# Second pass of a four-layer kernel: its first sequence written out ahead of the loop, weight pieces split inside that sequence's steps, twelve pieces staged ahead

## The chip, the core and the metric

The kernel runs on one core of one Trainium2 chip. The metric is the device time of one execution in microseconds (us), the median of several runs.

## What is computed

Eight sequences of 512 rows and 512 features pass through four layers one after the other: an adapter (layer 0), an attention block with a feed-forward part (layer 1), a feed-forward expert (layer 2) and a finite-difference step on the 512x512 grid that each sequence then is (layer 3). Cut to what matters here:

```python
# layer 1, behind the attention: x is (8, 512, 512)
h = _ln(x) * g2 + beta2
x = x + _gelu2(h @ W1 + b1) @ W2 + b2            # W1 512x2048, W2 2048x512, the same for all sequences
# layer 2: one of 8 experts for each sequence
h = gelu(x @ Wi[expert_idx] + bi)
r = h @ Wo[expert_idx] + bo + x
y = layer_norm(r) * gamma + beta
# layer 3: f = y as a grid
Af, Bf = A_grid * f, B_grid * f
df = -(grad(Af[0], 1) + grad(Af[1], 2)) + 0.5 * (grad2(Bf[0], 1) + grad2(Bf[1], 2) + ...)
out = maximum(f + df * dt, 0)
```

Matmuls of layers 1 and 2 are made with 16-bit operands: each float32 operand is split into a high and a low half (`_hi`, `_lo`), and each product is three matmuls (hi by hi, lo by hi, hi by lo; L1371 to L1373, 128x512 each).

## The kernel before, in words

**Two passes.** `attention_pass` runs layer 0 and the attention over all eight sequences (a hardware loop, L413 on SyncE) and stores its result `x2` to memory (`x_rows`). `ffn_pass` then runs the rest of layer 1, layer 2 and layer 3. Each pass is a block: all engines meet at its end. ScalarE, which issues the stores of `x2`, waits until all have landed (the last line of its part of the first pass) before it ends its block. Order of work on each engine is the order in which the code is written; engines wait for each other by semaphores.

**A sequence of the second pass** is 32 steps (`STEPS`, L1037), 16 of layer 1 (`n` below 16) and 16 of layer 2. In step `n` TensorE makes `up(n)` (12 matmuls into one of four banks), and then `down(n - 2)` (12 matmuls into the four accumulators; L1406 to L1444). ScalarE makes the gelu (L1512), VectorE splits its result into halves (L1686, L1687), which `down(n)` needs. Layer 2's weights come in 16 chunks of 512 KB: SyncE loads each into one of two buffers (L1257), ScalarE and VectorE split it (L1519, L1692) in steps 4, 6, 8 to 14 and later ones (`CHUNK`, L1044). In the middle of a sequence and at its end TensorE transposes the next activations (L1437, L1378).

**Layer 3 runs one sequence behind.** In the loop's body for sequence `it` the engines also normalise and difference the sequence before: `norm3`, `alpha` and `beta` on VectorE, grid products on GpSimd (L1298, L1305 to L1308), four times five matmuls on TensorE (`run_stencil`, L1423, L1357) and a store. So that the body is the same for every `it`, the first one does all of this on a tile `f` of zeros (memsets L1321, L1322), and its output rows are overwritten later. The last sequence's layer 3 stands behind the loop.

**Start of the second pass.** W1 and W2 are loaded in 16 pieces of 512 KB (`weight_pieces`). Four are loaded while the first pass ends, into slots 0 to 3 of a buffer `stage` of six slots (L442), and sequence 0's `x2` into slots 4 and 5 (L444). The second pass loads the vectors (L1241, L1243), normalises `x2` (L1554 to L1647), transposes it, and splits the 16 pieces ahead of the loop: high half on ScalarE (L1496), low half on VectorE (L1656). A slot is reloaded when its piece has been split (L1246). `up(0)` waits for four pieces and the split activations (L1394, L1402), `down(0)` for all sixteen (L1411):

```python
def down(n):
    k = n % NF
    if n == 0:
        pe.wait_ge(w_split, len(PIECES))
    pe.wait_ge(g_split, 1 + it * STEPS + n + 1)
```

GpSimd adds a bias to `x2` in four instructions (`move_x2`, L1312) as soon as the normalised rows are there. 24 matmuls on the identity (L1388) follow the first transposes on TensorE.

## Time and profile before

| | |
|---|---|
| median of 3 runs | 2598.64 us (2595.83 to 2599.11) |
| the profiled execution: time of the run | 2600.86 us |
| its span, first to last instruction | 2598.7 us |
| mean granted TensorE clock | 0.988 of full speed |
| busy: TensorE / VectorE / ScalarE / GpSimd | 2502.8 / 2011.6 / 1149.0 / 1050.5 us |
| first pass, second pass (by the block's end) | 0 to 1106 us, 1106 to 2598.7 us |

Times below are microseconds from the start of the span. A row of the timeline is: start, duration, engine, line, operation, output<-inputs with their shapes, count, and in brackets how long the engine had been idle before it and who released it. Matmuls are pipelined, so a row shows 0.38 us for one while they follow each other at some 0.216 us.

### The profile page before, as it was taken

The page shows a single profiled execution, that of the slowest core. Times are in us where ns is not written, and L with a number is a line of the kernel's source. Part 1 is how long each engine was busy: PE and PEld are TensorE (multiplying, and loading weights), DVE is VectorE, ACT ScalarE, POOL GpSimd, SP SyncE. Part 2 cuts the span into 40 slices and gives each one's busy share as a digit, 9 for nine tenths or more (in the row PEclk, how much of TensorE's full clock was granted, in tenths as well). Part 3 has the DMA queues.
Part 4 walks back from the last instruction along what each step waited for, and adds up shares of the span by engine and source line. Part 5 has one row for each costly group of instructions (what it writes and reads, how often), then busy time and mean ns, then how long its engine had stood idle before and what let it go on. Part 6 is the DMA issues. An engine that isn't in the chain of part 4 may idle for free.

```text
span 2598.7 us, 47184 instructions
## 1 busy us (share of the span) xinstructions
PE 2502.8 (96%) x14583; PEld 1240.8 (48%) x14583; DVE 2011.6 (77%) x3863; ACT 1149.0 (44%) x2189; POOL 1050.5 (40%) x887
## 2 busy tenths in 40 slices
PE   7999999999999999959999999999999999999997
PEld 5455555555555555534444444444444444444443
DVE  7777777777777777788868788688677886986787
ACT  3676767676767676733323222223232232232331
POOL 1464646464646464524324144143242350431330
PEclk8999999999999999979999999999999999999998
DMA  6444444445444444443222222242133222321440
GB/s 209 136 153 156 154 154 156 151 155 153 156 154 154 155 153 153 155 159 126 90 98 87 102 99 89 70 138 90 63 113 110 98 78 82 122 90 58 131 155 27
DMA packets 155507, 320.56 MB, mean 123 GB/s; under 512 B 17474, under 2 KB 23234, under 8 KB 155218
## 3 DMA queue, kind: packets, MB, share of 16 engines
q1 hardware_dynamic: 145426, 299.13, 35.1%
q10 hardware_dynamic: 9792, 17.83, 1.9%
q8 instruction: 151, 2.47, 0.4%
q14 instruction: 138, 1.13, 0.1%
HBM read 298.85 MB, written 17.86 MB: 122 GB/s over the span
## 4 chain that ended last, share of the span: by engine, by line
PE 51%; DVE 4%; issue 1%; ACT 1%; DMA 0%; DVEq 0%; ACTq 0%
PE ffn_bank L1371 16%; PE ffn_bank L1372 16%; PE ffn_bank L1373 16%; PE ffn_bank L1357 2%; DVE g2T_hi L1686 1%; PE ffn_bank L1437 1%; DVE g2T_lo L1687 1%; PE ffn_bank L1378 1%; DVE w_lo L1656 1%; DMA stage<-in_W 0%; PE ffn_bank L1466 0%; ACT g L1512 0%; DVE stage L1631 0%; DVE stage L1613 0%; DVE w_hi L1734 0%
## 5 line engine op out<-in xcount | busy, mean ns | idle before, releaser
L1000 DVE CUSTOM_DVE_ANT_0 tiles<-bank,stage 128x512 f32<-128x512 f32 x512 | 324.0, 687 | 81.1 <-PE bank L628 76.4
L792 ACT ACTIVATE tiles<-tiles,nmax 128x512 f32<-128x512 f32 x512 | 363.3, 713 | 47.1 <-DVE nmax L1000 47.0
L508 POOL TENSOR_TENSOR stage<-stage,mask_add 128x1024 f32<-128x1024 f32 x128 | 272.2, 2137 | 211.2 <-DMA stage<-in_bias 189.3
L651 PE MATMUL bank<-ident,tiles 128*128 128x128 f32 x2048 | 300.4, 280 | 18.9 <-ACT v L758 5.9
L1686 DVE CAST g2T_hi<-g 128x512 f16<-128x512 f32 x256 | 180.0, 703 | 176.7 <-ACT g L1512 169.3
L651 PEld LDWEIGHTS bank<-ident,tiles 128*128 128x128 f32 x2048 | 222.7, 140 | 179.5 <-issue 84.0
L1687 DVE TENSOR_TENSOR g2T_lo<-g,g2T_hi 128x512 f16<-128x512 f32 x256 | 259.6, 1014 | 8.8
L1298 POOL TENSOR_TENSOR stage<-grid,f 128x512 f32<-128x512 f32 x96 | 158.8, 1680 | 254.0 <-DVE f L1572 109.6
L1512 ACT ACTIVATE g<-ffn_bank,bi 128x512 f32<-128x512 f32 x128 | 87.9, 687 | 333.5 <-PE ffn_bank L1373 308.9
L778 ACT ACTIVATE pT<-bank 128x512 f32<-128x512 f32 x256 | 150.9, 589 | 152.1 <-PE bank L651 152.1
L1312 POOL TENSOR_TENSOR x<-x2n,b 128x512 f32<-128x512 f32 x32 | 39.5, 1269 | 439.3 <-DVE f L1714 439.3
L1371 PE MATMUL ffn_bank<-w_hi,g2T_hi 128*128 128x512 f16 x512 | 194.9, 381 | 14.6 <-DVE g2T_lo L1687 14.4
L1305 POOL TENSOR_TENSOR stage<-grid,f 128x512 f32<-128x512 f32 x64 | 96.1, 1521 | 268.1 <-DVE stage L1623 151.0
L1692 DVE SCALAR_TENSOR_TENSOR wl_lo<-stage,wl_hi 128x1024 f16<-128x1024 f32 x128 | 199.8, 1561 | 0.1
L1371 PE MATMUL ffn_bank<-x3T_hi,w_hi 128*128 128x512 f16 x512 | 194.0, 379 | 4.5 <-DVE x3T_lo L1653 3.4
L1371 PE MATMUL ffn_bank<-wl_hi,g2T_hi 128*128 128x512 f16 x512 | 194.1, 379 | 3.1 <-DVE g2T_lo L1687 3.1
L1372 PE MATMUL ffn_bank<-w_lo,g2T_hi 128*128 128x512 f16 x512 | 194.7, 380 | 0.0
L1373 PE MATMUL ffn_bank<-w_hi,g2T_lo 128*128 128x512 f16 x512 | 194.6, 380 | 0.0
L1371 PE MATMUL ffn_bank<-x3T_hi,wl_hi 128*128 128x512 f16 x512 | 194.2, 379 | 0.0
L1372 PE MATMUL ffn_bank<-wl_lo,g2T_hi 128*128 128x512 f16 x512 | 194.0, 379 | 0.0
L1373 PE MATMUL ffn_bank<-wl_hi,g2T_lo 128*128 128x512 f16 x512 | 194.0, 379 | 0.0
L1373 PE MATMUL ffn_bank<-x3T_hi,w_lo 128*128 128x512 f16 x512 | 194.0, 379 | 0.0
(289 smaller groups left out, 5230.5 us busy)
## 6 DMA issues: line engine op xcount, KB each, us to landing
stage<-in_bias SPq DMA_DIRECT2D x256, 512.0 KB, 4.3
stage<-in_W_l SPq DMA_DIRECT2D x128, 512.0 KB, 3.3
grid<-in_grids SPq DMA_DIRECT2D x160, 256.0 KB, 3.4
xin<-in_x SPq DMA_DIRECT2D x36, 256.0 KB, 4.0
out<-stage ACTq DMA_DIRECT2D x36, 256.0 KB, 2.0
x_rows<-tiles ACTq DMA_DIRECT2D x32, 256.0 KB, 3.0
stage<-in_W SPq DMA_DIRECT2D x16, 512.0 KB, 4.8
x2n<-x_rows SPq DMA_DIRECT2D x8, 1024.0 KB, 9.0
```

The lines of the kernel that those rows point to most:

```text
L508: pool.tensor_tensor(bias[:, n % NB, :, :], bias[:, n % NB, :, :], mask_add[:, u % T, :].unsqueeze(1).to_broadcast([P, 2, S]), ALU.add).th ...
L651: mm = pe.transpose(bank[:, t * P:(t + 1) * P], tiles[:, 4 * (u % NR) + i, t * P:(t + 1) * P], ident[:, :])
L778: act.activation(pT[:, (u // 2) % 2, i, :, (u % 2) * P:(u % 2 + 1) * P], bank[:, :].rearrange("p (t q) -> p t q", t=T), ACT.Copy).then_inc ...
L792: act.activation(tile, tile, ACT.Exp, scale=-1.0, bias=nmax[:, u % 2, i:i + 1], accum_out=rsum[:, j, h:h + 1]).then_inc(prob_ready, 1)
L1000: dve.tensor_tensor_reduce(tiles[:, 4 * (u % NR) + i, :], bank[:, :], bias[:, half % NB, i % 2, :], -1.0, 3.0e38, ALU.add, ALU.min, nmax[: ...
L1298: pool.tensor_tensor(prod[:, i, :], grid[:, i, :], f[:, t, :], ALU.mult).then_inc(alpha_prod, 1)
L1371: pe.matmul(out, w[0], x[0], start=first, stop=False)
L1372: pe.matmul(out, w[0], x[1], start=False, stop=False)
L1373: return pe.matmul(out, w[1], x[0], start=False, stop=last)
L1686: link(dve.tensor_copy(gT[0][:, n % 4, :], g32[:, n % 2, :]))
L1687: dve.tensor_tensor(gT[1][:, n % 4, :], g32[:, n % 2, :], gT[0][:, n % 4, :], ALU.subtract)\
L1692: dve.scalar_tensor_tensor(out=wl[1][:, k % NW, :], in0=raw[:, k % 2, :], scalar=WS, in1=wl[0][:, k % NW, :], op0=ALU.mult, op1=ALU.subtract)\
```

## The change

- The first sequence of the second pass is written out ahead of the loop, without layer 3 (there is no sequence before it); the loop runs over the other seven, with layer 3 of the sequence before. In place of each of the four `run_stencil` of the first sequence TensorE only signals the bank. The memsets of `f` and `l2_rows` go.
- Twelve pieces are staged ahead instead of four: 4 to 11 go into a buffer `late` of eight slots, the memory of the first pass's transposed probabilities `pT`, when the last product that reads those is done (`pv_done`). In the second pass the same memory holds `x2n`, `x2` and the halves `vsp`, `msp`.
- Before `up(0)` only pieces 0 to 3 are split. Pieces 4 and 5 are split in step 0, 6 to 15 in steps 1 to 10 (`PIECE_AT`), and `down(n)` waits only for the piece that it reads, `up(8)` for the first eleven. Pieces 12 and 13 are loaded into slots 2 and 3 of `stage`, pieces 14 and 15 into slots 4 and 5 when `move_x2` has read `x2` there.
- `move_x2` on GpSimd now waits until eight pieces are split, since its output lies in the slots of pieces 6 and 7.
- The vectors `g2`, `beta2`, `b1`, `dt`, `b2` and `idx` are loaded in the first pass, behind the first load of `ada` and ahead of its loop.

```diff
-NS = 4
+NS = 12
+PIECE_AT = {0: (4, 5), **{n: (n + 5,) for n in range(1, 11)}}
...
-    return w1[:C] + w2[:2] + w1[C:] + w2[2:]
-
-
-def staged(stage, i):
-
-    v = stage[:, i % NS, :]
-    return v.rearrange("p (k n) -> p k n", k=2) if C <= i < C + 2 or i >= 2 * C + 2 else v
-
-
-def attention_pass(nc, a, ada_rows, x2_dram, stage, stage_in):
+    return w1[:C] + w2[:2] + w1[C:C + 2] + w2[2:3] + w1[C + 2:] + w2[3:]
+
+
+def staged(stage, late, i, at):
+
+    v = stage[:, i, :] if i < C else late[:, i - C, :] if i < NS else stage[:, i - NS + 2, :]
+    return v if isinstance(at, tuple) else v.rearrange("p (k n) -> p k n", k=2)
+
+
+def staged_in(stage_in, i):
+
+    if i < NS:
+        return stage_in[i], 16
+    return stage_in[(2, 3, NS, 0)[i - NS]], 32
...
-        pT = sb("pT", [P, 2, 4, T, 2 * P], F32)
+        pT = late[:, :, :].rearrange("p (v i) (t q) -> p v i t q", v=2, t=T)
...
+            for dst, src in vectors(a, cols):
+                sp.dma_start(dst, src).then_inc(cols_in, 16)
...
-            for i, (src, _) in enumerate(weight_pieces(a)[:NS]):
-                sp.dma_start(staged(stage, i), src).then_inc(stage_in[i], 16)
+            pieces = weight_pieces(a)
+            for i in range(C):
+                sp.dma_start(staged(stage, late, i, pieces[i][1]), pieces[i][0]).then_inc(stage_in[i], 16)
             sp.wait_ge(x2_out, 1 + 64)
-            sp.dma_start(stage[:, NS:NS + 2, :].rearrange("p n (h s) -> p (n h) s", h=2),
+            sp.dma_start(stage[:, C:C + 2, :].rearrange("p n (h s) -> p (n h) s", h=2),
                          x2_dram[0].rearrange("(t p) d -> p t d", p=P)).then_inc(stage_in[NS], 16)
+            sp.wait_ge(pv_done, 1 + B * (NQ // 2))
+            for i in range(C, NS):
+                sp.dma_start(staged(stage, late, i, pieces[i][1]), pieces[i][0]).then_inc(stage_in[i], 16)
...
+        x2n, x2 = (late[:, i:i + 2, :].rearrange("p n (h d) -> p (n h) d", h=2) for i in (0, 2))
...
+        vsp, msp = ([late[:, i + j, :].bitcast(F16).rearrange("p (t d) -> p t d", t=T) for j in range(2)] for i in (4, 6))
...
-            for i, (src, _, _) in enumerate(PIECES):
-                if i >= NS:
-                    sp.wait_ge(w_split, i - NS + 1)
-                    sp.dma_start(staged(stage, i), src).then_inc(stage_in[i % NS], 16)
+            for i in range(NS, len(PIECES)):
+                if i < NS + 2:
+                    sp.wait_ge(w_split, i - NS + 3)
+                else:
+                    sp.wait_ge(x2b_ready, T)
+                signal, _ = staged_in(stage_in, i)
+                sp.dma_start(PIECES[i][1], PIECES[i][0]).then_inc(signal, 16)
             sp.dma_start(dmat[:, :, :], a["dmat"]).then_inc(dmat_in, 16)
             sp.dma_start(halo_w[:, :], a["halo"]).then_inc(dmat_in, 16)
-            sp.wait_ge(w_split, len(PIECES))
             sp.wait_ge(idx_clipped, 1)
-            with sp.Fori(0, B) as it:
-                e = sp.value_load(idx[0:1, bass.ds(it, 1)], min_val=0, max_val=NE2 - 1)
+
+            def sequence(it):
...
                 def load_rows():
-                    sp.wait_ge(f_ready, it * T + T)
+                    if not is_first(it):
+                        sp.wait_ge(f_ready, it * T)
                     sp.dma_start(bi[:, :], a["bi"][e]).then_inc(rows_in, 16)
                     sp.dma_start(l2_rows[:, :, :], a["rows2"][e].partition_broadcast(P)).then_inc(rows_in, 16)

                 def load_next_x2():
                     sp.wait_ge(x2b_ready, it * T + T)
+                    if is_first(it):
+                        sp.wait_ge(w_split, C + 2)
                     nxt = (it + 1) % B
...
+                loads += [(ALPHA[1], 2, load_rows, ()), (ALPHA[1], 3, load_next_x2, ())]
+                if not is_first(it):
+                    loads += [(ALPHA[t - 1] if t else -1, 1, stencil_load, (sp, it - 1, "alpha", t)) for t in range(T)]
+                    loads += [(BETA[t - 1] if t else ALPHA[-1], 1, stencil_load, (sp, it - 1, "beta", t)) for t in range(T)]
+                    loads += [(ALPHA[-1], 2, load_halo, ())]
...
+            sequence(0)
+            with sp.Fori(1, B) as it:
+                sequence(it)
...
-            pool.memset(f[:, :, :], 0.0).then_inc(zeroed, 1)
-            pool.memset(l2_rows[:, :, :], 0.0).then_inc(zeroed, 1)
             pool.memset(halo[:, :, :].rearrange("p t d -> p (t d)").bitcast(F32), 0.0).then_inc(zeroed, 1)
-            pool.wait_ge(vec_in, 16 * len(COLS))
+            pool.wait_ge(cols_in, 16 * len(cols))
             pool.wait_ge(h2_ready, T)
+            pool.wait_ge(w_split, 2 * C)
             for t in range(T):
                 move_x2(pool, x2_first, t)
...
-                    if n in (0, NF // 2):
-                        pe.wait_ge(w_split, C if n == 0 else 2 * C + 2)
+                    if is_first(it) and n in (0, NF // 2):
+                        pe.wait_ge(w_split, C if n == 0 else HALF_OF_W1)
...
-                    if n == 0:
-                        pe.wait_ge(w_split, len(PIECES))
+                    if is_first(it) and n in PIECE_OF_ROW:
+                        pe.wait_ge(w_split, PIECE_OF_ROW[n] + 1)
                     pe.wait_ge(g_split, 1 + it * STEPS + n + 1)
...
                     bank = claim(pe, it, ("L3", t))
-                    pe.wait_ge(alpha_done, it * T + T)
-                    pe.wait_ge(halo_in, it * 128 + 128)
+                    if is_first(it):
+                        pe.sem_inc(full_of(("L3", t)), 1)
+                        return
+                    pe.wait_ge(alpha_done, it * T)
+                    pe.wait_ge(halo_in, it * 128)
...
+            def piece_hi(i):
+                _, src, hi, _ = PIECES[i]
+                act.wait_ge(*staged_in(stage_in, i))
+                act.activation(hi, src, ACT.Copy, scale=WS).then_inc(w_hi, 1)
+
+            for i in range(C):
+                piece_hi(i)
+            act.wait_ge(cols_in, 16 * len(cols))
+            for c in range(C):
+                act.wait_ge(first_full, c + 1)
+                act.activation(xT[0][:, c, :], psum[c][:, :], ACT.Copy).then_inc(hi_done, 1)
+
...
+                    if is_first(it):
+                        for i in PIECE_AT.get(n, ()):
+                            piece_hi(i)
...
-            dve.wait_ge(idx_in, 16)
+            dve.wait_ge(cols_in, 16 * len(cols))
...
+            def piece_lo(i):
+                _, src, hi, lo = PIECES[i]
                 dve.wait_ge(w_hi, i + 1)
-                dve.scalar_tensor_tensor(out=lo, in0=staged(stage, i), scalar=WS, in1=hi,
-                                         op0=ALU.mult, op1=ALU.subtract).then_inc(w_split, 1)
-            dve.wait_ge(zeroed, 2)
-            before = links[0]
-
-            with dve.Fori(0, B) as it:
-                links[0] = 0
-                link = chained(it * LINKS_B + before)
-                prev = (it + (B - 1)) % B
+                dve.scalar_tensor_tensor(out=lo, in0=src, scalar=WS, in1=hi, op0=ALU.mult, op1=ALU.subtract).then_inc(w_split, 1)
+
+            piece_lo(0)
+            for c in range(C):
+                dve.wait_ge(hi_done, c + 1)
+                dve.tensor_tensor(xT[1][:, c, :], psum[c][:, :], xT[0][:, c, :], ALU.subtract).then_inc(h2T_split, 1)
+            for i in range(1, C):
+                piece_lo(i)
+
...
+                    if is_first(it):
+                        for i in PIECE_AT.get(n, ()):
+                            piece_lo(i)
...
+                    if not is_first(it):
+                        if n < 3:
+                            norm3(link, prev, n)
+                        if n in ALPHA:
+                            alpha(link, prev, ALPHA.index(n))
+                        if n in BETA:
+                            beta(link, prev, BETA.index(n))
...
+            sequence(0, link)
+            before = links[0]
+            with dve.Fori(1, B) as it:
+                links[0] = 0
+                sequence(it, chained((it - 1) * LINKS_B + before))
...
+        late = ctx.enter_context(nc.sbuf_tensor("late", [P, 8, 2 * D], F32))
```

**SyncE, from the last loads of the first pass over the block's end.** Before:

```order
L442 DMA stage<-in_W 128x1024 x4
L444 DMA stage<-x_rows 128x4x512
L153 UNCONDITIONAL_BRANCH
L1239 UNCONDITIONAL_BRANCH
L1241 DMA idx<-in_idx 1x8
L1243 DMA g<-in_g 128x512
L1243 DMA beta<-in_beta 128x512
L1243 DMA b<-in_b 128x16
L1243 DMA dt<-in_dt 128x8
L1243 DMA b<-in_b 128x512
L1247 DMA stage<-in_W 128x2x512 x2
L1247 DMA stage<-in_W 128x1024 x4
```

Now:

```order
L460 DMA stage<-in_W 128x1024 x4
L462 DMA stage<-x_rows 128x4x512
L466 DMA late<-in_W 128x2x512 x2
L466 DMA late<-in_W 128x1024 x2
L466 DMA late<-in_W 128x2x512
L466 DMA late<-in_W 128x1024 x2
L466 DMA late<-in_W 128x2x512
L168 UNCONDITIONAL_BRANCH
L1261 UNCONDITIONAL_BRANCH
L1269 DMA stage<-in_W 128x2x512 x4
L1270 DMA dmat<-in_dmat 128x1280
L1271 DMA halo_w<-in_halo 8x128
```

Eight of the twelve later pieces have moved ahead of the block's end (the two branches), the vectors have left this place, and four pieces stand ahead of the loads of `dmat` and `halo_w` and of the first chunks.

**VectorE, from the last normalised rows of sequence 0 (`h`) to the first steps.** Before:

```order
L1645 SCALAR_TENSOR_TENSOR h<-stage,mv,g 128x512
L1647 SCALAR_TENSOR_TENSOR h<-h,rstd,beta 128x512
L1656 SCALAR_TENSOR_TENSOR w_lo<-stage,w_hi 128x1024 x4
L1653 TENSOR_TENSOR x3T_lo<-ffn_bank,x3T_hi 128x512 x4
L1656 SCALAR_TENSOR_TENSOR w_lo<-stage,w_hi 128x1024 x12
L1661 UNCONDITIONAL_BRANCH
L1661 ISA
L1686 CAST g2T_hi<-g 128x512
```

Now:

```order
L1698 SCALAR_TENSOR_TENSOR h<-stage,mv,g 128x512
L1700 SCALAR_TENSOR_TENSOR h<-h,rstd,beta 128x512
L1705 SCALAR_TENSOR_TENSOR w_lo<-stage,w_hi 128x1024
L1710 TENSOR_TENSOR x3T_lo<-ffn_bank,x3T_hi 128x512 x4
L1705 SCALAR_TENSOR_TENSOR w_lo<-stage,w_hi 128x1024 x3
L1737 CAST g2T_hi<-g 128x512
L1738 TENSOR_TENSOR g2T_lo<-g,g2T_hi 128x512
L1705 SCALAR_TENSOR_TENSOR w_lo<-late,w_hi 128x1024 x2
L1737 CAST g2T_hi<-g 128x512
L1738 TENSOR_TENSOR g2T_lo<-g,g2T_hi 128x512
L1705 SCALAR_TENSOR_TENSOR w_lo<-late,w_hi 128x1024
```

The twelve splits that stood between the activations (`x3T_lo`) and the first gelu's halves (`g2T`) stand behind those halves, two in the first step and one in each of the next ten; three of the first four have moved behind the activations.

## Rows read from the trace of the kernel before

**Rows 1.** The page: busy time (share of the span) by engine.

```profile
PE 2502.8 (96%) x14583; PEld 1240.8 (48%) x14583; DVE 2011.6 (77%) x3863; ACT 1149.0 (44%) x2189; POOL 1050.5 (40%) x887
```

**Rows 2.** Waits of TensorE, 1155 to 2550: us in total, times, longest.

```profile
PE ffn_bank L1371 <- DVE g2T_lo L1687: 3.1, 8, 0.4
PE ffn_bank L1371 <- issue: 1.1, 4, 0.3
```

**Rows 3.** Timeline of TensorE at the start of the second pass.

```profile
1129.05 0.38 PE L1371 MATMUL ffn_bank<-x3T_hi,w_hi 128*128 128x512 f16 x1 [3.43 <-DVE x3T_lo L1653]
...
1136.60 0.38 PE L1373 MATMUL ffn_bank<-x3T_hi,w_lo 128*128 128x512 f16 x1
1151.42 0.60 PE L1371 MATMUL ffn_bank<-w_hi,g2T_hi 128*128 128x512 f16 x1 [14.43 <-DVE g2T_lo L1687]
...
1155.64 0.38 PE L1371 MATMUL ffn_bank<-x3T_hi,w_hi 128*128 128x512 f16 x1
```

**Rows 4.** Window there: length, TensorE busy (matmuls), granted clock, DMA share, GB/s.

```profile
1151.40:1155.00 3.60, 3.58 (x10) 0.54 0.97 341
```

**Rows 5.** Timeline of VectorE, from the block's end to the first gelu's halves.

```profile
1107.19 2.67 DVE L1639 TENSOR_SCALAR idx<-idx 1x8 int32<-1x8 int32 x1 [3.87 <-DMA idx<-in_idx]
...
1118.59 7.92 DVE L1656 SCALAR_TENSOR_TENSOR w_lo<-stage,w_hi 128x1024 f16<-128x1024 f32 x4
1126.44 2.47 DVE L1653 TENSOR_TENSOR x3T_lo<-ffn_bank,x3T_hi 128x512 f16<-128x512 f32 x4
...
1135.05 1.23 DVE L1656 SCALAR_TENSOR_TENSOR w_lo<-stage,w_hi 128x1024 f16<-128x1024 f32 x1 [1.59 <-ACT w_hi L1496]
...
1150.59 0.69 DVE L1687 TENSOR_TENSOR g2T_lo<-g,g2T_hi 128x512 f16<-128x512 f32 x1
```

**Rows 6.** Timeline of ScalarE: its four stores (ACTq), then the second pass's first operations.

```profile
1101.54 2.28 ACTq L808 DMA_DIRECT2D x_rows<-tiles  x4
1106.37 3.90 ACT L1496 ACTIVATE w_hi<-stage 128x1024 f16<-128x1024 f32 x4 [7.56 <-PEq L153]
1119.31 2.06 ACT L1494 ACTIVATE x3T_hi<-ffn_bank 128x512 f16<-128x512 f32 x4 [9.05 <-PE ffn_bank L1384]
...
1148.11 1.28 ACT L1512 ACT_TABLE_LOAD   x1
1149.41 1.27 ACT L1512 ACTIVATE g<-ffn_bank,b 128x512 f32<-128x512 f32 x2
```

**Rows 7.** Timeline of GpSimd, `move_x2` at the start.

```profile
1118.83 8.83 POOL L1312 TENSOR_TENSOR x<-stage,b 128x512 f32<-128x512 f32 x4 [8.08 <-DVE h L1647]
```

**Rows 8.** Groups of the page: busy us, mean ns of one | idle before: `move_x2` inside the loop.

```profile
L1312 POOL TENSOR_TENSOR x<-x2n,b 128x512 f32<-128x512 f32 x32 | 39.5, 1269 | 439.3 <-DVE f L1714 439.3
```

**Rows 9.** Timeline of TensorE: the last products that read `pT`.

```profile
1093.58 1.93 PE L642 MATMUL bank<-pT,v 128*32 128x256 f32 x32
```

**Rows 10.** DMA, 1100 to 1106 in 40 slices; then stores there, KB each, us to landing.

```profile
GB/s 0 0 0 0 0 0 0 0 0 0 0 0 0 0 0 68 300 382 410 382 355 382 410 382 355 383 410 382 328 410 396 410 341 396 110 0 0 0 0 0
...
x_rows<-tiles ACTq DMA_DIRECT2D x4, 256.0 KB, 2.1
```

**Rows 11.** DMA, 965 to 985 (end of sequence 6): stores beside loads.

```profile
x_rows<-tiles ACTq DMA_DIRECT2D x4, 256.0 KB, 3.6
xin<-in_x SPq DMA_DIRECT2D x4, 256.0 KB, 4.6
```

**Rows 12.** Timeline of VectorE in the middle of sequence 0: `x3`.

```profile
1226.67 2.58 DVE L1676 SCALAR_TENSOR_TENSOR x<-ffn_bank,x 128x512 f32<-128x512 f32 x4 [2.82 <-PE ffn_bank L1373]
```

**Rows 13.** Timeline of TensorE there: first `run_stencil`, then the transposes.

```profile
1228.32 0.38 PE L1357 MATMUL ffn_bank<-vsp_hi,dmat 128*128 128x512 f16 x1
...
1229.59 1.97 PE L1437 MATMUL ffn_bank<-ident,x 128*128 128x128 f32 x16
```

**Rows 14.** Timeline of SyncE near the first pass's start.

```profile
41.61 3.62 SPq L421 DMA_DIRECT2D stage<-in_bias  x6
```

**Rows 15.** Timeline of GpSimd: first use of a bias tile.

```profile
68.41 6.34 POOL L508 TENSOR_TENSOR stage<-stage,mask_add 128x1024 f32<-128x1024 f32 x3 [10.04 <-DVE mask_add L958]
```

141 lines of the change are left out of this document (67 added, 74 removed).

## The prediction

> **What bounds the kernel now.** First the page: TensorE is busy 96% of the span, no other engine over 77% [rows 1], so an edit elsewhere pays only where TensorE stands still or does work that needn't be done. Then TensorE's waits over nearly the whole second pass, 1155 to 2550: 4.2 us in all, none over 0.4 [rows 2]. So that pass is TensorE at full pace, and the change can win three things: an idle stretch at its start, the slow clock behind it, and matmuls of the first sequence that feed nothing. The timeline shows the first: `up(0)` to `up(2)` run from 1129.05 to about 1136.8, then TensorE is idle for 14.43 us until `down(0)` [rows 3]. Released by the halves of the first gelu, says the row; these were late because VectorE and ScalarE first split all sixteen pieces, the last of them near 1149 [rows 5, 6]. After the idle stretch the granted clock is 0.54, near the lower of its two levels (1.2 of 2.4 GHz) [rows 4], and `down(0)`, 12 matmuls, takes 4.22 us (1151.42 to 1155.64) [rows 3] where 12 take 2.59 at full pace: `up(0)` to `up(2)` are 36 in 7.77. Before `up(0)` stands a third stretch, from the block's end near 1106 to 1129, in which TensorE waits for VectorE.
>
> **The change, part by part.** I follow the first pass's end to `up(3)`, which starts at 1155.64 now [rows 3].
>
> *The block's end (a loss).* The eight loads into `late` start when the last product on `pT` is done, at 1095.5 [rows 9]. Their 4.19 MB move from about 1097.5 (the landing of a small transfer is 2 us behind its issue [rows 10], an estimate) at some 390 GB/s [rows 10]: alone they would end at 1108.2. But ScalarE's four stores of `x2` (1.05 MB) are issued from 1101.54 on [rows 6], ran alone from 1102.2 to 1105.3 [rows 10], and the block ends only when they have landed. Now 2.35 MB of loads are still under way at 1102.2. Bounds: the stores are not slowed (0), or wait for all loads (1108.2 + 2.7 = 1110.9, a loss of 5.6). Between lies equal sharing: 1.05 MB at 195 GB/s take 5.4 us instead of 3.1, a loss of 2.3. The nearest row is the end of sequence 6, where stores run beside loads of `x` and land in 3.6 us instead of 2.1 [rows 10, 11], a factor of 1.7, as equal sharing has it (5.4 / 3.1). I take 2.3. The Trainium skill's page "DMA: Bandwidth & Descriptors" (Queues, rings and completion order) speaks against this: a DMA engine takes turns between queues packet by packet, so the queue with the longer descriptors gets more; W1's rows here are 4 KB, those of the stores 2 KB, so the loss would be more than 2.3, up to about 5. No run here shows it yet.
>
> *From the block's end to `up(0)` (a gain).* VectorE now waits for `idx`, loaded behind the block's end, until 1107.19 [rows 5]; ScalarE began at 1106.37, moved by the stores at 1106.3 + 2.3 = 1108.6, and now VectorE begins with it, since the vectors are there. From there to the last normalised row is 11.4 us (1107.19 to 1118.6) [rows 5]: 1120.0. One split follows. The four first splits took 1.98 us each while `move_x2` ran on GpSimd [rows 5, 7]; undisturbed one takes 1.23 [rows 5], and `move_x2` now waits for piece 7. So 1121.3, then the activations' low halves, 2.47 [rows 5] (the high halves, 2.06 from 0.7 us behind the rows on [rows 6], are ready): 1123.8; three more splits: 1127.5; `up(0)` at 1127.7 instead of 1129.05. The 24 matmuls on the identity end before that.
>
> *`down(0)`.* Three `up` of 2.59: 1135.5 instead of 1151.42. It needs its piece: `up(0)` ends at 1130.3, table load 1.28 and gelu 0.64 [rows 6] to 1132.4, halves about 1.2 (gelu's end at 1150.0 to 1151.3 [rows 5, 6]) to 1133.7, then piece 4's low half, 1.23, to 1135.0: 0.5 us early. Its high half lies on ScalarE beside the gelu's halves. Gain 15.9. The idle stretch being gone, `down(0)` runs at full pace: 4.22 - 2.59 = 1.6. `up(3)` starts 17.5 earlier.
>
> *Steps 1 to 10.* TensorE needs 24 x 0.216 = 5.2 us for a step. VectorE: halves 1.2, a piece 1.23, in every second step a chunk of the same size 1.23: 3.7 at most. ScalarE: gelu 0.64, twice 1 us (3.90 / 4 [rows 6]). Both have cover; nothing is charged. The cover is 1.5 us a step, and what lacks it is a late transfer (rival 3).
>
> *Layer 3 of sequence 0.* Twenty matmuls go. One `run_stencil` with its gaps is 1.27 us (1228.32 to 1229.59) [rows 13]. The two late ones (behind `up(19)`, `up(20)`) are worth that: 2.5. The two in the middle filled waits: `x3` is ready at 1229.25 [rows 12], the transposes start at 1229.59 [rows 13], so the first yields 0.3, and the second, which covers the split of the transposed activations, as little (0.2). Together 3.0. VectorE's and GpSimd's share lay beside TensorE: nothing.
>
> *The vectors in the first pass.* Six issues of 0.6 us [rows 14] and 0.8 MB put the bias tiles back by some 4 us. These were issued by 45.2, and the first is read at 68.41, when the mask is ready [rows 14, 15]: cover of over 15 us, nothing. *Loop and branch*: bounds 0 and 0.4, the longest wait on issue in the pass [rows 2]; I take 0.
>
> **Sum:** 17.5 + 3.0 = 20.5. The profiled execution took 2600.86: 2580.4. It lies 2.2 above the median of the runs (2598.64), against which I state the forecast: **2578.1**.
>
> **Rivals.**
> 1. *The stores come last.* The loss at the block's end is the bound, 5.6 instead of 2.3: 2581.4. For it: the loads are all queued before the first store, and the page's rule of turns goes half of the way there. Against it: rows 11.
> 2. *The stores aren't slowed:* 2575.8. For it only that their queue is another.
> 3. *The first chunk is late.* SyncE now issues pieces 14 and 15 when `move_x2` is done, then `dmat`, `halo_w`, then chunk 0, which ScalarE wants in step 4, ahead of its next gelu. From `up(0)` on: piece 7 is split at 13, `move_x2` takes 5.1 alone [rows 8] to 8.8 beside VectorE [rows 7], five issues and a register load 3, data of 1.9 MB 5 to 7 with 2 us of start: it lands between 27 and 33. `down(5)` starts at 7.8 + 5 x 5.2 = 33.7, and the chunk's high half, gelu and halves before it take 3, so it stalls if the chunk is later than 30.6: up to 2.5 us, 2580.6.
> 4. *Steps 0 and 1 are late:* if ScalarE puts both pieces of step 0 and the table load in other order than I read it, `down(0)` waits 1 to 3 us: 2580.
> 5. *Slower than before.* The first sequence is now straight code and the loop is entered behind it. If each return of the loop and its entry stalled TensorE, seven times, by more than 20.5 / 7 = 2.9 us, the kernel would be slower: at 4 us each 2598.6 - 20.5 + 28 = 2606. Against it: the same loop returns now and waits on issue were 1.1 us in all [rows 2]. The Trainium skill ("Runtime: NRT & Kernel Launch", Instruction fetch mechanics) says that a taken branch whose target isn't in the loaded pages stalls for a fetch; by that rule each return of this long loop should stall, now as then, and the trace doesn't agree.
> 6. *It doesn't do what it says:* something else holds `down(0)` (SyncE's loads, GpSimd), and only the clock and layer 3 pay, some 4 us: 2594.
>
> **How the numbers follow.** Forecast as summed 0.42, rival 1 0.2, rival 2 0.08, rival 3 0.14, rival 4 0.08, rival 5 0.03, rival 6 0.05. The bounds reach from 2575.8 to, with rivals 1 and 3 together and a late step, 2586; below, the runs scatter by 2 or 3 us (2595.83 to 2599.11), which gives 2573. A measurement of this kernel can tell about 0.2%, 5.2 us, from no change; all cases but 5 and 6 lie beyond it on the fast side, and rival 6 (4.6 us) within it: faster 0.92, same 0.05, slower 0.03.
>
> **What would show it.** Right: TensorE's idle stretch before the first matmul on `w_hi,g2T_hi` is gone or under 1 us; the granted clock in `down(0)` is full; in sequence 0 no matmul on `dmat`; the two middle stretches show idle times near 1 us; the stores of the last sequence land later, with the first operation of the second pass near 1108.6; `w_lo` of the first four pieces 1.23 us each; `up(3)` near 1138. Wrong: a first operation of the second pass behind 1111 (rival 1), a wait of ScalarE for a chunk in step 4 (rival 3), waits of TensorE on issue over 1 us at each return (rival 5), an idle stretch of over 10 us still before `down(0)` (rival 6).

## The result and the profile after

| | us |
|---|---|
| kernel before, beside the changed one | 2597.89 median of 4 (2595.83 to 2599.11) |
| changed kernel | 2578.53 median of 4 (2578.06 to 2578.86) |
| ratio | 0.9926, 95% interval 0.9909 to 0.9943 |
| profiled execution of the changed kernel | 2578.06, span 2576.2 |
| forecast | 2578.1, range 2573 to 2586 |

The time fell by 19.4 us between the medians and by 22.8 between the profiled executions (2600.86 and 2578.06). That is within half a microsecond of the forecast, and in part luck: one term of its sum, a loss, was 5.6 us too small, and beside a second profiled execution of the kernel before (run e10 below) the change is worth 16.6 us, not the 20.5 of the sum. The 22.8 include about 6 us that belong to the first profiled execution and not to the change.

First the page of the changed kernel, busy time by engine, to be laid beside [rows 1], and of its DMA queues the one that carries instructions (packets, MB, share of 16 engines), which was 151 packets before:

```profile
PE 2485.8 (96%) x14475; PEld 1236.3 (48%) x14563; DVE 1951.3 (76%) x3756; ACT 1140.3 (44%) x2177; POOL 997.1 (39%) x857
...
q8 instruction: 95, 1.56, 0.2%
```

The busy time of TensorE can't be laid beside [rows 1] as it stands. Its 14475 matmuls are 88 fewer than its 14563 weight loads: records of matmuls of the first pass (out of 256 on `mask_add` this trace has 168) are missing. The kernel of e1_later below, which makes the same matmuls and has all 14563 in its trace, has 2490.0 us, the kernel before 2502.8 and 2497.9 in its two traces: 8 to 13 us less, not 17. The waits of TensorE from `up(3)` of the first sequence to 2530 answer to [rows 2] (engine, line, releaser: us, times, longest):

```profile
PE ffn_bank L1406 <- DVE g2T_lo L1738: 2.7, 7, 0.4
PE ffn_bank L1406 <- DVE x3T_lo L1719: 1.2, 1, 1.2
PE ffn_bank L1475 <- DVE late L1727: 0.8, 1, 0.8
```

The second and third are the two stretches in the middle of the first sequence that the stencils filled; waits on issue are gone. The timeline of TensorE answers to [rows 3], the window behind it to [rows 4] (length, busy, granted clock, DMA share, GB/s):

```profile
1121.93 6.63 PE L1423 MATMUL ffn_bank<-ident 128*128 128x128 f32 x48
1128.40 0.38 PE L1406 MATMUL ffn_bank<-x3T_hi,w_hi 128*128 128x512 f16 x1
...
1136.17 0.38 PE L1406 MATMUL ffn_bank<-w_hi,g2T_hi 128*128 128x512 f16 x1
```

```profile
1136.10:1138.80 2.70, 2.70 (x15) 1.00 0.00 0
```

`down(0)` stands directly behind `up(2)`, with no wait, at the upper level of the clock: the 14.43 us and the slow matmuls of [rows 3, 4] are gone. The next two fences are VectorE and ScalarE at the same place, answering to [rows 5, 6]:

```profile
1109.74 0.22 DVE L1693 TENSOR_SCALAR idx<-idx 1x8 int32<-1x8 int32 x1 [11.20 <-PEq L168]
...
1120.88 1.22 DVE L1705 SCALAR_TENSOR_TENSOR w_lo<-stage,w_hi 128x1024 f16<-128x1024 f32 x1
1122.22 2.48 DVE L1710 TENSOR_TENSOR x3T_lo<-ffn_bank,x3T_hi 128x512 f16<-128x512 f32 x4
1124.62 3.48 DVE L1705 SCALAR_TENSOR_TENSOR w_lo<-stage,w_hi 128x1024 f16<-128x1024 f32 x3
1131.91 0.43 DVE L1737 CAST g2T_hi<-g 128x512 f16<-128x512 f32 x1 [3.80 <-ACT g L1558]
...
1132.98 2.35 DVE L1705 SCALAR_TENSOR_TENSOR w_lo<-late,w_hi 128x1024 f16<-128x1024 f32 x2
```

```profile
1096.76 2.43 ACTq L829 DMA_DIRECT2D x_rows<-tiles  x4
1109.53 3.89 ACT L1534 ACTIVATE w_hi<-stage 128x1024 f16<-128x1024 f32 x4 [15.50 <-PEq L168]
```

The split of pieces 4 and 5 now stands behind the first gelu's halves, inside step 0. But from the issue of the first store to the first operation of the second pass there are now 12.8 us, where [rows 6] have 4.8.

Marks that both timelines have give the whole difference, and the same marks in e10's execution of the kernel before show which of it belongs to the change:

| stretch, us | before | changed | difference | before, again | difference to that |
|---|---|---|---|---|---|
| start to the first store of the last `x2` | 1101.54 | 1096.76 | -4.8 | 1097.03 | -0.3 |
| to ScalarE's first operation of the second pass | 4.83 | 12.77 | +7.9 | 4.83 | +7.9 |
| to `up(3)` of the first sequence | 49.27 | 29.23 | -20.0 | 48.96 | -19.7 |
| to the first transposition of `h` (L1378, L1413) | 157.93 | 154.30 | -3.6 | 157.78 | -3.5 |
| to the end | 1285.13 | 1283.14 | -2.0 | 1284.20 | -1.1 |
| span | 2598.7 | 2576.2 | -22.5 | 2592.8 | -16.6 |

The forecast had: -17.5 for the second and third line together with a loss of 2.3 in it, -3.0 for the fourth, nothing for the first and last.

### The profile page after: what moved, and what is told of

Read it like the earlier page. It is cut to its first block, busy times and chain, and to the rows that moved or that the text cites. A ratio compares the mean times of both kernels' runs of the same rounds, so it can differ in the third digit from the quotient of the medians.

```text
span 2576.2 us, 46724 instructions
## 1 busy us (share of the span) xinstructions
PE 2485.8 (96%) x14475; PEld 1236.3 (48%) x14563; DVE 1951.3 (76%) x3756; ACT 1140.3 (44%) x2177; POOL 997.1 (39%) x857
## 4 chain that ended last, share of the span: by engine, by line
PE 52%; DVE 3%; issue 1%; ACT 0%; DVEq 0%; ACTq 0%
PE ffn_bank L1406 16%; PE ffn_bank L1408 16%; PE ffn_bank L1407 16%; PE ffn_bank L1392 1%; PE ffn_bank L1475 1%; PE ffn_bank L1413 1%; DVE g2T_hi L1737 1%; DVE g2T_lo L1738 0%; PE ffn_bank L1423 0%; DVE w_lo L1795 0%; DVE w_hi L1795 0%; DVE stage L1685 0%; ACT g L1558 0%; DVE stage L1666 0%; PE ffn_bank L1508 0%
## 5 line engine op out<-in xcount | busy, mean ns | idle before, releaser
L672 PE MATMUL bank<-ident,tiles 128*128 128x128 f32 x2048 | 300.2, 280 | 16.6 <-ACT late L799 4.3
L1738 DVE TENSOR_TENSOR g2T_lo<-g,g2T_hi 128x512 f16<-128x512 f32 x256 | 243.4, 951 | 8.8
L1342 POOL TENSOR_TENSOR late<-late,b 128x512 f32<-128x512 f32 x32 | 39.5, 1266 | 464.0 <-DVE f L1769 464.0
L1328 POOL TENSOR_TENSOR stage<-grid,f 128x512 f32<-128x512 f32 x84 | 141.0, 1704 | 197.7 <-DVE f L1625 75.3
L799 ACT ACTIVATE late<-bank 128x512 f32<-128x512 f32 x256 | 151.0, 590 | 149.9 <-PE bank L672 149.9
L1407 PE MATMUL ffn_bank<-x3T_lo,w_hi 128*128 128x512 f16 x512 | 194.1, 379 | 0.0
L1407 PE MATMUL ffn_bank<-x3T_lo,wl_hi 128*128 128x512 f16 x512 | 194.1, 379 | 0.0
```

The source lines that it names most:

```text
L672: mm = pe.transpose(bank[:, t * P:(t + 1) * P], tiles[:, 4 * (u % NR) + i, t * P:(t + 1) * P], ident[:, :])
L799: act.activation(pT[:, (u // 2) % 2, i, :, (u % 2) * P:(u % 2 + 1) * P], bank[:, :].rearrange("p (t q) -> p t q", t=T), ACT.Copy).then_inc ...
L1328: pool.tensor_tensor(prod[:, i, :], grid[:, i, :], f[:, t, :], ALU.mult).then_inc(alpha_prod, 1)
L1407: pe.matmul(out, w[0], x[1], start=False, stop=False)
L1738: dve.tensor_tensor(gT[1][:, n % 4, :], g32[:, n % 2, :], gT[0][:, n % 4, :], ALU.subtract)\
```

## The experiments

The kernel before runs beside each group; its medians there were 2595.45, 2595.86 and 2596.77 us.

**Who holds the block's end?** The eight loads into `late` move from the end of the first pass to the start of the second.

```diff
-            sp.wait_ge(pv_done, 1 + B * (NQ // 2))
-            for i in range(C, NS):
-                sp.dma_start(staged(stage, late, i, pieces[i][1]), pieces[i][0]).then_inc(stage_in[i], 16)
...
         @block.sync
         def _(sp):
+            for i in range(4, NS):
+                sp.dma_start(PIECES[i][1], PIECES[i][0]).then_inc(stage_in[i], 16)
```

> Theory (the eight loads that are queued ahead of the four stores of x2 hold these, and through them the block's end): with the eight loads issued by SyncE at the start of the second pass, the stores land about 2 us behind their issue, the first operation of the second pass stands 4.6 us behind the first store's issue as in the kernel before (instead of 12.5), and the time falls by 8 us against the changed kernel, to 2570.5 us. The pieces then land from 10 to 12 us behind the block's end, well ahead of the first split of piece 4 (over 25 us behind it). Rival A (the end of the block is late for another reason, the stores are slow whatever is queued): no change, 2578.5. Rival B (the loads now meet the start of the second pass and the first operations or piece 4 are late): 2573 to 2578, with a wait of ScalarE or VectorE for a DMA on a piece.

Measured: 2570.60 us (2570.24 to 2571.05), ratio to before 0.9902 (0.9887 to 0.9917). The stores land as in the kernel before; this is the DMA of that run from 1094 to 1104 (KB each, median us to landing), and behind it ScalarE's first operation:

```profile
late<-in_W SPq DMA_DIRECT2D x6, 512.0 KB, 7.1
x_rows<-tiles ACTq DMA_DIRECT2D x4, 256.0 KB, 2.1
```

```profile
1096.90 2.28 ACTq L826 DMA_DIRECT2D x_rows<-tiles  x4
1101.72 3.90 ACT L1533 ACTIVATE w_hi<-stage 128x1024 f16<-128x1024 f32 x4 [7.55 <-PEq L168]
```

4.82 us instead of 12.77, and no engine waits for a piece, so rivals A and B fall. The time is the expected one to 0.1 us, but with some luck: from the first operation to `up(3)` this kernel takes 29.91 us instead of 29.23, since the matmuls on the identity now hold `up(0)` back, the spans of the two profiled executions lie 7.0 us apart, and the kernel before was 2.4 us faster beside this group than beside the changed kernel. In the changed kernel the DMA from 1094 to 1112 reads:

```profile
q1 hardware_dynamic: 1383, 3.65, 58.6%
q10 hardware_dynamic: 576, 1.05, 15.1%
issues: line engine op xcount, KB each, median us to landing
late<-in_W SPq DMA_DIRECT2D x3, 512.0 KB, 11.9
x_rows<-tiles ACTq DMA_DIRECT2D x4, 256.0 KB, 9.0
```

**How does the loss depend on what is queued?** The same with four of the eight loads ahead (`range(C, 8)` in the first pass, `range(8, NS)` in the second).

> Only pieces 4 to 7 (2.1 MB) are loaded ahead of the block's end, 8 to 11 at the start of the second pass. Theory (the stores land when all that is queued ahead of them is through): 2.1 MB from 2 us behind the first issue at 390 GB/s are through about when the stores are issued, so the first operation comes 5 to 6 us behind the first store's issue and the time is 2571 to 2572 us. Rival (a queue's share is fixed, and the loss is 8 us as soon as any loads are under way beside the stores): first operation over 9 us behind the stores' issue, 2575 us or more.

Measured: 2572.03 us (2571.46 to 2572.29); the first operation comes 6.93 us behind the first store's issue, 2.1 later than with none and 5.8 earlier than with eight. The loss is no fixed share: with half of the bytes ahead it is a quarter. I had said 5 to 6 us, so it is 1 us larger than the theory's figure; the time stands at the upper end of the expected 2571 to 2572.

How the eight hold the stores is seen by queue in the changed kernel, first from 1102 to 1104, then from 1104 to 1106 (packets, MB, share; q1 carries the loads, q10 the stores):

```profile
q1 hardware_dynamic: 150, 0.54, 66.1%
q10 hardware_dynamic: 153, 0.28, 36.4%
```

```profile
q1 hardware_dynamic: 194, 0.46, 58.4%
q10 hardware_dynamic: 191, 0.36, 46.2%
```

The queues take turns packet by packet, 150 to 153 and 194 to 191, and the loads' packets are larger (0.54 MB in 150 is 3.6 KB, 0.28 in 153 is 1.8 KB). That is the rule of the Trainium skill that the prediction named (page "DMA: Bandwidth & Descriptors", Queues, rings and completion order), and here the trace agrees. But it is half of the loss only. From the first store's issue at 1096.76 to 1100 no packet of q10 moves, from 1100 to 1102 there are 30 of its 576: about 4.5 us pass ahead of the turns (4.5 in e5_after_again, 1.1 in e2_half), where 0.8 do in the kernel before [rows 6, 10]. And the loads were slower than the 390 GB/s of the sum, as these two windows from 1096 to 1100 show (length, clock, DMA share, GB/s):

```profile
1096.00:1098.00 2.00, 1.00 0.98 291
1098.00:1100.00 2.00, 1.00 0.82 224
```

The slow stretch isn't the stores' doing: in e1_later, where none run, the same loads have 229 and 253 GB/s from 1106 to 1110, between 409 and 417 before and behind. It lies where the third and fourth of the eight loads are under way (they land at 1098.5 and 1101.2 here, at 1108.3 and 1111.0 there). What causes it, and what holds the first packets, is open.

**Do the vectors matter?** The changed kernel with `idx` and the five vectors loaded at the start of the second pass; and the kernel before with only their move into the prologue.

```diff
             load_ada(0)
-            for dst, src in vectors(a, cols):
-                sp.dma_start(dst, src).then_inc(cols_in, 16)
...
         @block.sync
         def _(sp):
+            vecs = vectors(a, cols)
+            for dst, src in vecs[-1:] + vecs[:-1]:
+                sp.dma_start(dst, src).then_inc(idx_in if dst is vecs[-1][0] else cols_in, 16)
```

> The changed kernel with idx and the five vectors loaded at the start of the second pass again, as before. If the load of the vectors in the prologue is what makes the first pass 4.8 us shorter (by the place of the bias tiles in time), the first pass is as long as in the kernel before and the time is 2578.5 + 4.8 + 0.8 = 2584 us. If the shorter first pass comes from where the tiles of the first pass now lie, or is scatter between executions, the first pass keeps its 2.3 us of the seven later sequences, and only VectorE's wait for idx comes back at the start of the second pass, 0.8 us to 2 us: 2579.3 to 2580.5 us.

> The kernel before with the vectors and idx loaded in the prologue and nothing else of the change. If this load shortens the first pass by 4.8 us: 2597.9 - 4.8 - 0.8 = 2592.3 us, and the last x2 row of the first pass near 1096 us. If it does nothing there: 2596 to 2597.5 us (only the wait for idx at the start of the second pass goes, 0.8 to 2 us), and the last x2 row between 1098 and 1101 us.

Measured: 2579.61 us (2578.61 to 2580.53) for the first, and 2595.22 (2593.95 to 2597.03, 11 runs) against 2595.45 for the second, ratio 0.9999 (0.9990 to 1.0008). In the changed kernel the vectors' place is worth 1.1 us: from the first operation to `up(3)` 30.35 us instead of 29.23. In the kernel before it gives nothing that can be told: `up(0)` stands 22.72 us behind ScalarE's first operation there, and 22.68 in the kernel before. And the first pass doesn't depend on it: the last sequence's first `x2` row starts at 1096.34 with the vectors moved and 1096.55 with them put back. So 1100.69 in the first profile of before asked for another cause.

**Was the profiled execution of before typical?** Both kernels once more.

> The kernel before, profiled again. Theory (4.8 us of the first pass and 2.0 us of the seven later sequences of the second pass in its first profiled execution are scatter of that execution, not the change): the first x2 row of the last sequence starts at 1095 to 1098 us instead of 1100.7, the seven sequences of the second pass take 175.25 us each instead of 175.25 to 175.72, and the span is 2592 to 2595 us; then the change by itself is worth 16 to 17.5 us. Rival (both belong to the kernel before): 1100 us or more, 1228.6 us for the seven sequences, span near 2598.

> The changed kernel once more, on the chip of the other runs. Theory (of the 22.8 us between the two profiled executions, the 4.8 us of the first pass are scatter of the profiled execution of the kernel before, which lay 3 us above its median): the last x2 row of the first pass starts at 1098 +- 1 us, as in the kernel before with the vectors moved (1098.3), the time is 2578 to 2579.5 us and the gain against the kernel before on the same chip 17 to 18 us. Rival (the change really shortens the first pass): last x2 row near 1096, gain over 20 us.

Measured: before 2596.56 us (2594.65 to 2600.16, 11 runs), its profiled execution 2594.65, span 2592.8; changed 2576.58 (2576.48 to 2578.64), ratio 0.9924 (0.9910 to 0.9937). The first `x2` row of the last sequence starts at 1096.18 in the former and 1095.72 in the latter, and between 1094.5 and 1097.2 in all thirteen profiled executions other than the first. So the first pass isn't shorter by the change; the 4.8 us were that execution. e10's own profiled execution was the fastest of its eleven runs, 1.9 us below their median, so the 16.6 us of the table are at the low end. Of the 4.8 us, 4 x (1 - 0.57) = 1.7 are one stretch near its start in which the clock was granted low, in the kernel before and then in the changed one:

```profile
86.00:90.00 4.00, 4.00 (x18) 0.57 0.30 111
```

```profile
86.00:90.00 4.00, 4.00 (x24) 1.00 0.10 35
```

e3_vec_back and e11_no_filler show the same dip there, the others don't: it comes and goes between executions. The rest is spread over the sequences (129.5 to 130.2 us each against 128.9 to 130.0 elsewhere).

The seven later sequences of the second pass were expected at 175.25 us each and took 175.23 to 175.50 in e10: there only a part of the 2.0 us is scatter. A rival that I hadn't stated had to be found, and the first idea was TensorE's three waits, which the change takes out of the loop.

**Is the loop shorter because three waits left it?**

```diff
-                    if is_first(it) and n in (0, NF // 2):
+                    if n in (0, NF // 2):
                         pe.wait_ge(w_split, C if n == 0 else HALF_OF_W1)
...
+                    elif n == 0:
+                        pe.wait_ge(w_split, len(PIECES))
```

> The changed kernel with TensorE's three waits on the split pieces (ahead of up(0), up(8) and down(0)) back inside the loop; they are always fulfilled there. Theory (the loop's sequences are 0.3 us shorter each because these instructions are gone): the distance from the first to the last transposition of h (1228.2 in the changed kernel, 1230.3 in the kernel before) is 1230.3 again, TensorE waits on issue 1.1 us ahead of up(0), and the time rises by 2.1 us, to 2580.6. Rival (the 2.1 us come from elsewhere): 1228.2 and 2578.5 us.

Measured: 2578.20 us (2577.49 to 2579.26), and the seven sequences stay at 175.23 to 175.26. The theory fell. What tells the kernels apart is the queue that carries instructions. From 1300 to 2500 it moved, in e10_before_again, in the changed kernel and in e11_no_filler (below), in this order:

```profile
q8 instruction: 62, 1.02, 0.4%
```

```profile
q8 instruction: 6, 0.10, 0.0%
```

```profile
q8 instruction: 59, 0.97, 0.3%
```

All kernels with 6 or 7 packets there (nine of them) run the seven sequences in 175.23 to 175.27 us each. The five with 59 or 62 (before, its two relatives, e11 and e12) have sequences of up to 175.72, 175.37, 175.50, 176.32 and 175.58. So the kernel before moves instructions in every round of its second loop, some nine packets a round, and its rounds are 0.1 to 2.0 us longer in all; the changed one moves none behind the first round. That the packets cost this time is argued and not shown by a run that changes them alone, but the place fits. In e11 the wait on issue ahead of `up(0)` comes back once a round, behind the first, for 3.6 us in all; three of the six rows of TensorE's timeline are

```profile
1645.36 0.38 PE L1406 MATMUL ffn_bank<-x3T_lo,w_hi 128*128 128x512 f16 x1 [0.41 <-issue]
1821.47 0.38 PE L1406 MATMUL ffn_bank<-x3T_lo,w_hi 128*128 128x512 f16 x1 [0.43 <-issue]
2349.98 0.38 PE L1406 MATMUL ffn_bank<-x3T_lo,w_hi 128*128 128x512 f16 x1 [0.46 <-issue]
```

176 us or three times that apart, each of the six 2.3 to 2.7 us behind a packet of this queue. The kernel before has four such waits, of 0.2 to 0.3 us, at the same place of its rounds and 2.6 to 2.7 us behind a packet. Where the code lies seems to decide it: e11 differs from e7_chunkwise, a kernel with 6 packets, only by 12 matmuls ahead of the loop. The page "Runtime: NRT & Kernel Launch" of the Trainium skill (Instruction fetch mechanics) has such a stall for a taken branch. These waits agree with it, and the nine quiet kernels don't: their loop is as long and returns as often without a packet. The prediction set the stall aside because waits on issue were 1.1 us; that was about its size in that execution, and a cost of the kernel before that went.

**Is it the split inside the steps, or the staging?** All pieces split ahead of the first sequence, the twelve staged pieces kept.

```diff
-PIECE_AT = {0: (4, 5), **{n: (n + 5,) for n in range(1, 11)}}
+PIECE_AT = {}
...
-            for i in range(1, C):
+            for i in range(1, len(PIECES)):
                 piece_lo(i)
```

(ScalarE's high halves likewise, behind those of the activations.)

> The changed kernel with all sixteen pieces split ahead of the first sequence on ScalarE and VectorE, as before; the twelve staged pieces stay. Theory (the split ahead of the first gelu is what made TensorE idle, not the loading): pieces 14 and 15 land near 1145, VectorE ends its splits at 1147 to 1148, down(0) starts at 1149 to 1150 with the clock at the lower level, up(3) near 1153.5 instead of 1138.8: 2593 us. Rival (the loading alone was the limit, as the pieces waited for a free stage buffer): 2580 to 2584 us.

Measured: 2597.80 us (2596.03 to 2599.01), ratio to before 1.0003 (0.9994 to 1.0013). From the first operation to `up(3)` it takes 48.82 us, as the kernel before (48.96, 49.27). VectorE and TensorE there:

```profile
1138.27 2.35 DVE L1707 SCALAR_TENSOR_TENSOR w_lo<-stage,w_hi 128x1024 f16<-128x1024 f32 x2
1149.87 2.53 DVE L1707 SCALAR_TENSOR_TENSOR w_lo<-stage,w_hi 128x1024 f16<-128x1024 f32 x2 [9.25 <-ACT w_hi L1534]
```

```profile
1154.43 0.59 PE L1406 MATMUL ffn_bank<-w_hi,g2T_hi 128*128 128x512 f16 x1 [16.88 <-issue]
1154.81 0.63 PE L1407 MATMUL ffn_bank<-w_lo,g2T_hi 128*128 128x512 f16 x1
```

The idle stretch is back, and the 12 matmuls of `down(0)` take 5.07 us again, 0.42 each. Staging more pieces without the new order brings nothing here, and the 8 us of held stores eat more than the other edits bring. The time is 4.8 us above what I expected; pieces 14 and 15 landed at 1148.8 and 1150.1 instead of 1145. But the run doesn't separate order from loading as it was meant to. Of the idle stretch some 9 us are a wait for these two pieces (ScalarE 14.10 us, VectorE 9.25 in the row above), which SyncE may load only when `move_x2` has read their slots, and that took GpSimd 11.40 us here, until 1145.4. Without this wait `down(0)` would have started some 9 us earlier (an estimate). So with both kernels staged alike, the order decides, by 19.6 us up to `up(3)` (48.82 against 29.23): `down(0)` needs piece 4 alone and the late pieces are hidden behind matmuls. Whether the new order with four staged pieces would do was not tried.

**What are the stencils of the first sequence worth?** The same twenty matmuls in the same four places, on other operands, their results unused.

```diff
                     if is_first(it):
-                        pe.sem_inc(full_of(("L3", t)), 1)
+                        pe.wait_ge(zeroed, 1)
+                        pe.wait_ge(dmat_in, 32)
+                        for k in range(4):
+                            pe.matmul(bank[:, :], dmat[:, 5 * (k // 2), :], w2[k % 2][:, t, :], start=k == 0, stop=False)
+                        pe.matmul(bank[:, :], halo_w[:, :], halo[:, t, :], start=False, stop=True).then_inc(full_of(("L3", t)), 1)
                         return
```

> The changed kernel with TensorE's share of layer 3 back in the first sequence: the same twenty matmuls in the same four places, on other operands (rows of the second weight in place of the products), the results unused. Theory: the two in the middle cost 0.5 us together, since TensorE waits 1.2 + 0.8 us there, and the two late ones 1.27 us each by the prediction, 1.55 us each by the two traces (3.1 us); the first transposition of h comes 3.6 us later than in the changed kernel, counted from up(3) (157.9 instead of 154.3 us), and the time rises by 3.0 to 3.6 us. Rival (layer 3 was fully covered and the 3.6 us come from somewhere else): no change.

Measured: 2582.61 us (2581.55 to 2583.86), 4.1 above the changed kernel's median and 6.0 above e5's; from `up(3)` to the first transposition of `h` 157.21 us instead of 154.30 in the trace, which is 2.9. The prediction's 3.0 stands; of the 3.6 of the table, 0.7 is something else, and fetching, which the first sequence of before does as well, is a guess.

**What bounds the start now?** In e1_later the last low half of the first four pieces ends at 1120.3 and `up(0)` starts at 1121.27, behind the matmuls on the identity. First `up(0)` waits for one piece at a time, with 12 of these matmuls ahead and 4 between its groups; then without the fillers; then without the 12 too.

```diff
-            for _ in range(24):
-                pe.matmul(psum[7][:, 0:P], ident[:, :], ident[:, :], start=True, stop=True)
+            warm(12)
...
                             else:
                                 pe.wait_ge(h2T_split, it * C + C)
+                            if is_first(it) and n == 0:
+                                pe.wait_ge(w_split, c + 1)
...
                         mm = three(bank[:, :], w, [x[:, c, :] for x in xT], c == 0, c == C - 1)
+                        if is_first(it) and n == 0 and c < C - 1:
+                            warm(4)
```

> The kernel e1_later, with up(0) of the first sequence waiting for one piece ahead of each group of three matmuls instead of for all four, and 12 matmuls on the identity ahead of it and 4 between two groups. In e1_later the last low half of the four pieces is done at 1120.3 and up(0) starts only at 1121.3, behind the 24 matmuls on the identity. Theory: up(0) now ends 0.65 us behind the last low half, at 1121.0 instead of 1123.86, 2.9 us less, and if nothing else is late the time is 2567.7 us. Rival (the granted clock, which rose during the 24 matmuls, rises later, and up(0) to up(2) run in part at the lower level): 1 to 3 us given back, 2569 to 2571 us.

> The kernel e7_chunkwise without the three groups of 4 matmuls on the identity inside up(0); the 12 ahead of it stay. In e7 the fourth group of up(0) starts at 1122.96 although its piece is split at 1119.81, so the fillers hold it. Theory: up(0) ends at 1121.0 instead of 1123.6 and the time is 2567.4 us, 2.7 us under e7. Rival (without the fillers TensorE pauses between the groups and the granted clock falls back or rises later): 2569 to 2571 us, with a granted clock below 1 behind 1119.

> As e11_no_filler, and without the 12 matmuls on the identity ahead of up(0). Theory (the clock rises only some 9 us behind the first of the transpositions, if TensorE is kept busy from there): TensorE pauses from 1113.6 to 1117.5, up(0) runs at the lower level, 0.43 us a matmul, and the level rises near 1126; up(0) to up(2) take 4 to 5 us more than at full pace: 2571 to 2572 us. Rival (the transpositions alone bring the clock up, and the matmuls on the identity cost only their time): 2567 us or less.

Measured: 2570.06 us (2568.70 to 2570.77), 2573.47 (2572.76 to 2574.51) and 2570.67 (2568.52 to 2571.31), against 2570.60 of e1_later. From the first operation to `up(3)` they take 30.16, 27.14 and 28.25 us against 29.91. So the first gains nothing, since the fillers hold `up(0)`'s groups back. The second gains the 2.8 us that were expected, at full clock, and loses more than that later:

```profile
PE ffn_bank L1406 <- issue: 3.6, 6, 0.9
```

Its loop fetches instructions again, and from the first transposition of `h` to the end it takes 1288.31 us where 1283.3 is the rule. The third runs its first twelve matmuls at the lower level (a start every 0.43 us), with the clock rising near 1120.7:

```profile
1116.00:1120.50 4.50, 4.50 (x12) 0.50 0.32 117
1121.00:1124.00 3.00, 3.00 (x16) 1.00 0.40 154
```

and is still 1.7 us earlier at `up(3)` than e1_later, but 1.1 later than e11: 12 matmuls on the identity are worth 1.1 us there. That is no comparison of 24 with none, since e12 also starts `up(0)` with the first piece, 3.3 us ahead of the end of the fourth's split. I had expected the lower level to cost `up(0)` to `up(2)` 4 to 5 us, with the rise near 1126; it cost 2.6 (10.37 instead of 7.77). Its loop fetches as well (0.7 us). A version with e11's start and the quiet loop would be at about 2570.6 - 2.8 = 2567.8, an estimate; it wasn't tried. The best that was measured is e1_later, e7 and e12, which can't be told from one another at 2570 to 2571: 1% under the kernel before (ratios 0.9902, 0.9896 and 0.9899) and 0.3% under the changed one.

## Why the prediction was right, and where it wasn't

- **The idle stretch and the clock** (15.9 and 1.6). Right, each step: `down(0)` 7.77 us behind `up(0)`, at full clock, with piece 4 split at 1134.2 (1132.98 + 1.22), 2.0 early instead of 0.5, since the table load stood ahead of `up(0)`. e8, with the old order, has the idle stretch and the slow matmuls again, though half of the stretch there is a wait for late pieces. "The 24 matmuls on the identity end before that" is wrong by a little: they end at 1128.56, directly ahead of `up(0)`, 0.3 us behind the last split. From the first operation to `up(3)` the forecast had 29.5 us (1108.6 to 1138.1), the trace 29.23.
- **The block's end.** This is the step that failed: "Between lies equal sharing: [...] a loss of 2.3. [...] I take 2.3", with 5.6 as the far bound. It is 7.9 us, beyond the bound. Two things were wrong in the bound's working: the loads run at 224 to 291 GB/s for 4 us, not at 390, and the stores' first packets wait about 4.5 us before the queues take turns at all. The nearest row [rows 11] had 1.05 MB of stores and 1.9 MB of loads in 20 us; it says nothing of stores that find 2.7 MB queued ahead. e1 and e2 settle it: 0, 2.1 and 7.9 us for none, four and eight loads ahead. Rival 1 had the mechanism, and too small a price.
- **Layer 3 of the first sequence** (3.0). e9 measures 2.9 in the trace. In the middle 2.0 us of waits replaced the stencils, as expected.
- **The vectors** (nothing in the first pass). Right. At the start of the second pass they are worth 1.1 us.
- **The first chunk** (rival 3). ScalarE waits 4.3 us for it, from 1148.4 to 1152.67, 24.3 us behind `up(0)`, where the prediction had 27 to 33 and a stall behind 30.6. TensorE doesn't wait. The wait is where the prediction put it, and it is covered.
- **The loop and its fetches** (rival 5, "bounds 0 and 0.4"). The sign was wrong: the change takes fetches away. The quiet loop is worth 2.0 us against the first profiled execution, 1.1 against the second and 0.1 against e4.
- **The baseline.** The sum was set against a profiled execution of 2600.86 us and then put on the median, 2.2 lower. The 4.8 us of that execution's first pass and the excess of its second loop are in no term of the sum, so they didn't make the number right; the median of three runs (2598.64) was 0.75 above the one measured beside the changed kernel, and hid as much of the error. Against e10 the change is worth 16.6 us of span, 4 less than the sum of 20.5 (by the table: 5.7 less in the second and third line, 0.5 more in the fourth, 1.1 in the last, 0.3 in the first: 16.7). Between medians it is 19.4 and 19.3 us, with intervals that reach from 15 to 24; the 2 or 3 us between these and the 16.6 aren't settled. They may be what the kernel before loses in most of its executions, whose times spread over 3 to 5.5 us where the changed kernel's spread over 1 to 2.

So the place and nearly all sizes were right, the loss was taken 5.6 us too small, and the number was still met: some 1.9 us came from the other lines of the table, 0.75 from the median that the forecast stood on, and 2.8 from medians that lie further apart than the marks of e10 have it, for a reason that is open. That part is luck.

## What to carry to other kernels

A block whose end waits for stores must not queue its next stage's loads ahead of them: put the loads behind the end if they are needed late enough (here the first of them was read 22 us behind it), and read from the trace by queue when the first packet of the store moves. Take the marks of a second profiled execution before a term is booked to a change; here some 6 of 22.5 us were the execution's. And look at the packets of the instruction queue inside a loop: where every round has some, the same code a few instructions further on may run without.

## What was not expected of the hardware

- Four stores of 256 KB issued with 2.7 MB of loads still queued on another queue moved no packet for 4.5 us, then had every second packet; they landed 9.0 us behind their issue instead of 2.1.
- The same loop of the second pass costs 175.23 to 175.27 us a round when the instruction queue is quiet, and up to 1.1 us more in single rounds when it moves some nine packets of 16 KB a round; between e7 and e11 12 matmuls ahead of the loop decided which.
- In e12 the granted clock rose near 1120.7, some 13 us behind the first transposition, where TensorE had paused for 2.7 us in between, and in e1 near 1118, 9 us behind it, with matmuls on the identity in the pause. The lower level cost `up(0)` to `up(2)` 2.6 us in e12; the 24 matmuls on the identity, which were to prevent it, held `up(0)` back by 1 us in e1.
- Two of the pieces moved at 224 to 291 GB/s (229 and 253 in e1) with the engines of the DMA busy for 0.8 of the time and more, between others at over 400, with stores waiting beside them and without.
